# The lists of a mixture-of-experts layer: the stores of finished tiles move to ScalarE's queue, and the expert's register is loaded earlier

## The reference, cut to what matters

```python
res_hidden = jnp.einsum('bsi,ri->bsr', x, A)                 # 64 numbers per row
combine = jnp.sum(jax.nn.one_hot(topi, num_experts) * topw[..., None], axis=-2)
delta = jnp.einsum('bse,bsr,eor->bso', combine, res_hidden, B)   # 16 experts, 1024 outputs
return base_out + delta * SCALING
```

## Time and profile before

| what | value |
|---|---|
| median of 3 runs | 1404.12 us (1402.51 to 1405.16) |
| the profiled execution's own time | 1402.49 us |
| span from the first to the last instruction of it | 1400.7 us |
| mean granted clock of TensorE | 0.977 |
| list stage, first product to last copy | 582.29 to 744.63 us |

### The profile page before, as it was taken

The page is one execution under the profiler, slowest core; times in us unless marked ns, Lnnn a source line. Parts: engine busy times, 40 slices in busy tenths (PEclk is TensorE's granted clock), DMA queues, the critical chain, the costliest instruction groups (busy, mean ns, idle before and its releaser), DMA issues.

```text
span 1400.7 us, 22809 instructions
## 1 busy us (share of the span) xinstructions
PE 1301.7 (93%) x7255; PEld 1150.2 (82%) x7256; DVE 808.9 (58%) x2057; ACT 329.4 (24%) x745; POOL 376.6 (27%) x335
## 2 busy tenths in 40 slices
PE   6999999999999999488884799999999999999998
PEld 5999999999999999255553588888888888888887
DVE  6556677666666664544443755565555655555642
ACT  4212222211111120333332322222222222222221
POOL 1212222222322322000004544433344333444200
PEclk9999999999999999699996899999999999999999
DMA  7234433333333332577778423323333333233100
GB/s 279 90 97 137 138 128 113 107 103 98 101 112 114 98 98 71 191 286 294 287 292 313 149 91 120 113 97 120 107 103 120 100 110 120 90 120 114 66 30 30
DMA packets 69133, 187.10 MB, mean 134 GB/s; under 512 B 8705, under 2 KB 25473, under 8 KB 68994
## 3 DMA queue, kind: packets, MB, share of 16 engines
q1 hardware_dynamic: 55424, 147.79, 30.2%
q0 software_dynamic: 11264, 37.76, 8.3%
q10 hardware_dynamic: 2418, 1.23, 0.3%
HBM read 106.00 MB, written 80.74 MB: 133 GB/s over the span
## 4 chain that ended last, share of the span: by engine, by line
PE 84%; DVE 8%; issue 4%; DMA 2%; ACT 1%; ACTq 1%; POOL 1%; DVEq 0%; POOLq 0%; SPq 0%
PE z L1153 22%; PE z L1155 21%; PE z L1154 21%; PE c L1153 5%; PE c L1155 5%; PE c L1154 5%; PE t L1225 2%; PE t L1194 2%; DVE onehot L857 1%; DMA w_1raw<-in_w_dram 1%; DVE yl L813 1%; DVE x8l L796 1%; PE t L1314 1%; DVE bl L909 1%; PE prep L1371 1%
## 5 line engine op out<-in xcount | busy, mean ns | idle before, releaser
L1153 PE MATMUL z<-w_1h,yh 128*128 128x384 f32 (+1 forms) x512 | 194.1, 379 | 0.0
L1154 PE MATMUL z<-w_1h,yl 128*128 128x384 f32 (+1 forms) x512 | 188.7, 369 | 0.0
L1155 PE MATMUL z<-w_1l,yh 128*128 128x384 f32 (+1 forms) x512 | 188.7, 369 | 0.0
L1153 PE MATMUL z<-w_0h,yh 128*128 128x384 f32 (+1 forms) x512 | 187.2, 366 | 0.0
L1155 PE MATMUL z<-w_0l,yh 128*128 128x384 f32 (+1 forms) x512 | 187.2, 366 | 0.0
L1154 PE MATMUL z<-w_0h,yl 128*128 128x384 f32 (+1 forms) x512 | 187.0, 365 | 0.0
L813 DVE TENSOR_TENSOR yl<-t,yh 128x512 fp32r<-128x512 f32 x128 | 82.3, 683 | 178.9 <-ACT yh L601 178.9
L1153 PE MATMUL z<-w_2h,yh 128*128 128x336 f32 (+1 forms) x512 | 153.2, 299 | 4.9 <-DVE yl L813 3.6
L1154 PE MATMUL z<-w_2h,yl 128*128 128x336 f32 (+1 forms) x512 | 152.8, 299 | 0.0
L1155 PE MATMUL z<-w_2l,yh 128*128 128x336 f32 (+1 forms) x512 | 152.8, 299 | 0.0
L601 ACT ACTIVATE yh<-t 128x512 fp32r<-128x512 f32 x128 | 69.5, 595 | 256.9 <-PE t L1225 165.5
(11 more groups left out here) (210 smaller groups left out, 2606.1 us busy)
## 6 DMA issues: line engine op xcount, KB each, us to landing
zs_dram<-zt SPq DMA_DIRECT2D x80, 512.0 KB, 2.7
x8raw<-in_x_dram SPq DMA_DIRECT2D x32, 516.0 KB, 4.1
xin<-in_x_dram SPq DMA_DIRECT2D x32, 512.0 KB, 3.3
x_dram<-xb SPq DMA_DIRECT2D x32, 512.0 KB
out_dram<-xb SPq DMA_DIRECT2D x32, 512.0 KB, 2.9
xin<-x_dram SPq DMA_DIRECT2D x16, 512.0 KB, 3.9
x<-x_dram SPq DMA_DIRECT2D x16, 512.0 KB, 3.7
ht<-hs_dram SPq DMA_DIRECT2D x80, 64.0 KB, 2.0
```

Source lines behind the costliest of these rows:

```text
L1153: T.matmul(o, ah, wh, start=start, stop=False, **kw)
L1154: T.matmul(o, al, wh, start=False, stop=False, **kw)
L1155: return T.matmul(o, ah, wl, start=False, stop=stop, **kw)
```

## The change: what it does, with the diff

The wait for the two halves of `zt` and the store leave SP's program and stand in ACT's, behind ACT's own copy of the left half. SP keeps the loads of rows. In PE's program the `value_load` of `tab_pair` moves from just ahead of the products to the first place of the tile's step, ahead of the turn of tile j + 1 and of all waits.

```diff
@@ SP
-            def listed_out_and_in(i, v, more=True):
+            def next_ht(i, v):
                 j = 4 * i + v
-                if more:
-
-                    sp.wait_ge(ht_ps, j + 1)
-                    load_ht(j + 4, v)
-                sp.wait_ge(zt_act, j + 1)
-                sp.wait_ge(zt_dve, j + 1)
-                sp.dma_start(zs_t[j], zt[v][:, :]).then_inc(zs_out[v], 16)
+                sp.wait_ge(ht_ps, j + 1)
+                load_ht(j + 4, v)
...
             for v in range(4):
-                listed_out_and_in(0, v)
+                next_ht(0, v)
             with sp.Fori(1, LISTED // 4 - 1) as i:
                 for v in range(4):
-                    listed_out_and_in(i, v)
-            for v in range(4):
-                listed_out_and_in(LISTED // 4 - 1, v, more=False)
-
+                    next_ht(i, v)
@@ ACT, outputs(i, v)
                 copy(zt[v][:, 0:HALF], (z[0], cp[0])[v % 2][:, :]).then_inc(zt_act, 1)
+                act.wait_ge(zt_act, j + 1)
+                act.wait_ge(zt_dve, j + 1)
+                act.dma_start(zs_t[j], zt[v][:, :]).then_inc(zs_out[v], 16)
@@ PE, listed_products(i, v)
                 j = 4 * i + v
+                k = pe.value_load(tab_pair[0:1, j, :], min_val=0, max_val=KC - 1)
                 if not last:
                     if v == 3:
                         turn_ht(i + 1, 0)
...
                     pe.wait_ge(zt_dve, j - 1)
-                k = pe.value_load(tab_pair[0:1, j, :], min_val=0, max_val=KC - 1)
```

## The result

The changed kernel takes 1407.43 us (median of 20 runs, 1404.29 to 1409.76), the kernel before 1404.15 (20 runs, 1402.51 to 1408.04). The ratio is 1.0022, with a 95% interval of 1.0015 to 1.0029: slower by 3.1 us by the ratio, 3.3 by the medians. The forecast was 1406.0. The profiled execution has a span of 1403.8 us against 1400.7, at the same mean clock of 0.977.

What follows compares the result with a forecast made beforehand. PE's late sequencer, with its register load, was taken to bound the loop at 2.024 us per tile. -0.9 + 1.2 + 1.6 = +1.9 us gave 1404.4 on the profiled execution, 1406.0 against the median; range 1399.5 to 1412.5.

Steps and rivals of the forecast that it cites:

- What bounded the kernel before: List-tile loop: PE's sequencer comes late, with 42.8 us of issue waits over 69 tiles, at 2.024 us per tile.
- the load's 0.31 us: PE's sequencer: loading the expert's register takes 0.31 us, most of the 0.88 us from hl to products with register operations.
- PE's own ring: Loop after the change: DVE's copy, hl, products and next copy take 0.09 + 0.14 + 1.70 = 1.93 us per tile.
- The first tile, -0.9: Start of the stage: products start about 0.14 us behind the first hl instead of 1.02, saving 0.9 us once.
- The closed ring, 2.04 us a tile: Loop: DVE's copy, ACT's store, ACT's hh, DVE's hl, DVE's next copy set a pace of 2.04 us per tile.
- The term of the sum: Loop of 72 tiles: pace rising from 2.024 to 2.04 us per tile costs +1.2 us.
- The static tiles: Tiles at both ends of the stage: without address operations, they come out within 0.2 us of before.
- The end of the stage, +1.6: Last store: sharing the engines with the earlier-issued x1-row loads doubles its 1.64 us transfer, costing +1.6 us.
- the bound of 4.9: End of stage, rival: all three x1-row loads go ahead of the last store, 4.9 instead of 1.6, 1409.3 us; chance 0.09.
- The doubling: Last store's 512 KB: engines serve queues in turn, so the store gets every second turn and 1.64 us doubles.
- The sum: Whole kernel: first tile -0.9, loop +1.2 and end of stage +1.6 give +1.9 us.
- the Trainium skill's floor: PE's register load: the page's floor of about 0.6 us would make the first tile win 1.2 us instead of 0.9.

Runs made afterwards that it cites:

- without the load the kernel with the ring cut: Expert pair 0 for every tile, no register loaded, in the kernel that issues each store behind the next tile's hh: 1380.01 us, ratio 0.9837.
- the register load alone: Kernel before with only the register load moved to the front of PE's step, stores still on SP: 1401.88 us, ratio 0.9983.
- the two experiments on it: Changed kernel with each store split into two issues of 64 rows, 1466.13 us; changed kernel with expert pair 0 for every tile, 1404.63 us.
- no register load: Changed kernel with expert pair 0 for every tile, so no register is loaded: 1404.63 us, ratio 1.0003.
- the run without the lead: Changed kernel with SP issuing the three x1-row loads only once the last tile's copies are done: 1405.23 us, ratio 1.0012.
- the store alone: Changed kernel with the register load put back behind the waits, just ahead of the products, stores still on ACT: 1454.0 us, ratio 1.0348.
- hh ahead of the store: Changed kernel with ACT issuing the store of tile j - 1 behind hh of tile j + 1: 1402.47 us, ratio 0.9985.

## Why the prediction was nearly right, point by point

**What bounded the kernel before.** Probably right in kind: PE's sequencer, with the register load. The wait ahead of the products is there, and without the load the kernel with the ring cut, whose copies wait for PE as before, gained 0.29 us a tile; no run took it out of the kernel before itself. But the prediction took the load's 0.31 us for a fixed price, and moving the load changed its length. With the 1.93 us that the prediction gave PE's own ring, the register load alone would have been worth 6.8 us in the loop and 0.9 at the first tile; it gave 2.4.

**The first tile, -0.9.** Right: products 0.15 us behind the first hl, 0.87 saved.

**The closed ring, 2.04 us a tile.** Right as a mechanism, and the two experiments on it agree (0.79 us more issue, 0.75 more pace; no register load, no gain). Its terms came out as: copy 0.69 as forecast; to the issue 0.21 for 0.24; issue 0.34 for 0.39; to hh 0.17 for 0.16, without the branch; hh and its gap 0.31 as forecast; hl to the next copy 0.21 for 0.20. That is 1.93 us. Three turns of four take that in the trace; the one at the end of the loop's pass takes 2.26, which is 0.08 more on average and makes the 2.013. The term of the sum was +1.2 us; the loop measured -0.74. The issue was mis-sized most, by taking the longer 64 KB stores of ACT as the nearest row.

**The static tiles.** "Within 0.2 us of before" was wrong at the front, by +0.63 us in the first four tiles: about half is the ring, which the sum priced for the loop alone, and half the lower clock at the stage's start, which it left out.

**The end of the stage, +1.6.** This is the step that failed: +4.2 us, near the bound of 4.9 that stood as a rival with little chance. The doubling itself is right where both queues start together (4.89 us). The prediction saw that the loads would be out 0.7 us ahead, and priced that lead at nothing: it gave the store every second turn from its issue on. The first load was out 0.79 us ahead, the second some 0.4 us (their two issues together take 0.85), the third 0.10 us behind the store's issue. The store moved nothing until 4.10 us behind its issue, 3.25 us later than a store in the loop, and then shared; it landed after 7.16 us, 2.3 us later than in the run without the lead. Three other runs with a lead of 0.78 to 0.79 us (the store alone, hh ahead of the store, no register load) landed it after 7.25 to 7.40 us. Why a lead of 0.79 us costs that stays open; no run varied it.

**The sum.** -0.87 + 0.63 - 0.74 + 0.23 + 4.22 = +3.5 us, against +3.3 between the medians and +1.9 forecast. Two errors, of -1.9 in the loop and +2.6 at the end, partly cancelled, so that the number came this near is in part luck.

**The register load and its page.** The prediction set 0.31 us against the Trainium skill's floor of about 0.6 us for such a load (DMA: Bandwidth & Descriptors, Latency and other measured facts) and let the trace decide. The runs show both: 0.30 us where no store's packets move, 0.5 to 1.0 where they do. The page's figure is no floor here, but it is nearer to the loads that fall into a store's transfer than the one that the prediction used. For SP's loads, which the prediction also puts at 0.31, the median before was 0.27.

## What to carry to other kernels

A store that is moved to a busy engine's queue puts not only its issue (0.34 us) but also its wait into that engine's order; look at what stands behind it, and issue it behind the small operation on which the next tile depends (5 us here). An order between transfers that one queue kept by itself is gone when they are split over two: a store that someone waits for should not be overtaken by loads that nobody needs yet (some 4 us here). And a limit that is removed is worth only the distance to the next one: 0.06 us a tile for the ring, then 0.29 for the register loads.

## What the runs showed of the hardware

A sequencer's load of one register from a table is no constant. In the changed kernel's loop the packets of a store move from 0.85 to 2.26 us behind its issue (medians). PE's loads that began within 0.5 us of the latest issue took 0.31 us there, those that began 1.5 to 2.0 us behind it 0.54, those later still 0.31 (medians). When the store was cut to an eighth, all but one took 0.30 to 0.31. SP's own loads of the row table show it as well, before, after the change, and with the store alone:

```profile
L426 SPq TENSOR_LOAD <-tab_row x80: 262/268/842, 574.2 to 736.5; - x80
```

```profile
L426 SPq TENSOR_LOAD <-tab_row x80: 265/632/992, 573.4 to 731.0; - x80
```

```profile
L426 SPq TENSOR_LOAD <-tab_row x80: 263/276/842, 574.6 to 775.0; - x80
```

The last two kernels have the same program on SP and on ACT, and medians of 0.63 and 0.28 us: what differs is how far behind the latest store's issue the loads of the loop fall, 0.9 to 1.6 us in the first, and 2.2 to 2.5 for every second one in the other. And an issue for 64 rows of 4 KB took 0.49 us on ACT, one for 128 rows 0.34.
